# The first and third expert stage begin before the last six sequences are routed

## What is computed

```python
logits = x @ router_w
top_vals, top_idx = jax.lax.top_k(logits, K)          # K = 2 of 8 experts
importance = jax.nn.softmax(top_vals, axis=-1)
gate = jax.nn.silu(jnp.einsum('th,ehf->etf', x, w1))  # layer 1: F = 256
up = jnp.einsum('th,ehf->etf', x, w3)
expert_out = jnp.einsum('etf,efh->eth', gate * up, w2)
...
h = jax.nn.gelu(x @ W1[e] + b1[e])                    # layer 2: F = 512
y = h @ W2[e] + b2[e]
...
x = x + 0.5 * ffn0(layernorm(x));  x = x + attention0(layernorm(x));  x = x + 0.5 * ffn0(layernorm(x))
x = x + 0.5 * ffn1(x);             x = x + attention1(x);             x = x + 0.5 * ffn1(x)
```

## Time and profile before

| What | us |
|---|---|
| median of 3 runs (3025.21 to 3033.71) | 3025.9 |
| span of the profiled execution | 3022.4 |

### The profile page before, as it was taken

The page is one execution under the profiler, slowest core; times in us unless marked ns, Lnnn a source line. Parts: engine busy times, 40 slices in busy tenths (PEclk is TensorE's granted clock), DMA queues, the critical chain, the costliest instruction groups (busy, mean ns, idle before and its releaser), DMA issues.

```text
span 3022.4 us, 74232 instructions
## 1 busy us (share of the span) xinstructions
PE 2350.3 (78%) x24646; PEld 1530.8 (51%) x24646; DVE 2147.5 (71%) x6077; ACT 1635.4 (54%) x3371; POOL 1531.1 (51%) x1644
## 2 busy tenths in 40 slices
PE   2328958999999588532699489999999999958990
PEld 1217746777777477422588323333333333327880
DVE  3636657778776467686577488888888888846775
ACT  1116634555555366311577247777767667747770
POOL 4770034666653477577100555566565653145871
PEclk9999978999999799755799679999999999979995
DMA  8123323223322244332322111111111111012226
GB/s 171 43 64 104 104 68 88 81 79 80 84 79 59 57 116 119 98 96 71 90 87 84 60 47 40 39 49 52 40 47 47 47 37 44 19 33 77 86 85 177
DMA packets 250053, 222.84 MB, mean 74 GB/s; under 512 B 67078, under 2 KB 230668, under 8 KB 249164
## 3 DMA queue, kind: packets, MB, share of 16 engines
q1 hardware_dynamic: 216028, 148.82, 17.9%
q0 software_dynamic: 33664, 69.27, 7.6%
HBM read 114.00 MB, written 107.53 MB: 73 GB/s over the span
## 4 chain that ended last, share of the span: by engine, by line
PE 53%; POOL 14%; DVE 8%; issue 8%; ACT 4%; DMA 4%; SPq 1%; POOLq 0%; DVEq 0%; ACTq 0%
PE PS L525 10%; POOL choice_outputs L1116 8%; PE PS L705 8%; PE PS L529 6%; PE PS L674 6%; PE PS L653 6%; PE PS L616 5%; POOL slot_inputs L1107 4%; DVE xr L1268 3%; PE PS L723 2%; ACT arena L854 2%; PE PS L657 2%; PE PS L661 2%; DVE mxs L1494 2%; PE PS L682 1%
## 5 line engine op out<-in xcount | busy, mean ns | idle before, releaser
L964 ACT ACTIVATE arena<-PS 128x512 f32<-128x512 f32 (+1 forms) x1344 | 699.1, 586 | 284.7 <-PE PS L674 163.2
L1494 DVE TENSOR_REDUCE mxs<-PS 128x1 f16<-128x512 f32 x1024 | 650.6, 685 | 113.3 <-PE PS L653 103.4
L1107 POOL DMA_INDIRECT slot_inputs<-xs,slots x512 | 510.4, 997 | 414.1 <-PE PS L674 211.2
L1173 POOL DMA_INDIRECT G<-block_outputs,places x256 | 253.8, 991 | 654.7 <-DMA block_outputs<-arena 424.2
L653 PE MATMUL PS<-w,q 96*128 96x512 f16 x1024 | 398.8, 391 | 31.7 <-DVE mxs L1494 30.1
L674 PE MATMUL PS<-q,w 100*128 100x512 f16 x1024 | 390.6, 384 | 18.4 <-ACT arena L964 18.3
L1116 POOL DMA_INDIRECT choice_outputs<-arena x284 | 325.8, 1147 | 131.3 <-issue 83.0
L854 ACT ACTIVATE arena<-PS 128x256 f16<-128x256 f32 (+2 forms) x586 | 257.6, 440 | 225.4 <-PE PS L529 165.3
L529 PE MATMUL PS<-ident,arena 128*128 128x128 f32 x1084 | 204.1, 290 | 157.3 <-DMA arena<-slot_inputs 107.9
L1498 DVE TENSOR_REDUCE mxs<-PS 128x2 f16<-128x320 f32 x512 | 243.0, 492 | 117.3 <-PE PS L661 112.4
L1432 DVE TENSOR_TENSOR arena<-PS,arena 128x256 f16<-128x256 f32 x284 | 120.4, 424 | 238.0 <-ACT arena L854 238.0
(11 more groups left out here) (192 smaller groups left out, 4277.5 us busy)
## 6 DMA issues: line engine op xcount, KB each, us to landing
arena<-slot_inputs SPq DMA_DIRECT2D x284, 129.0 KB
block_outputs<-arena SPq DMA_DIRECT2D x142, 128.0 KB, 1.7
qk_parts<-qk SPq DMA_DIRECT2D x64, 256.0 KB, 2.4
G<-choice_outputs SPq DMA_DIRECT2D x64, 256.0 KB
q<-qk_parts SPq DMA_DIRECT2D x128, 96.0 KB
slot_inputs<-xs,slots POOLq DMA_INDIRECT x512, 2.4
qk_parts<-qk SPq DMA_DIRECT2D x64, 128.0 KB, 2.5
W<-qk_parts SPq DMA_DIRECT2D x128, 48.0 KB
```

The source lines that it names most:

```text
L964: activate(pT[:, u % PTR, 0:n], PS[:, SC0 + u % NSC[a], 0:n], ACT.Exp, scale=SCALE).then_inc(s_pe, 1)
L1107: g.indirect_dma_start(Xs, bass.IndirectOffsetOnAxis(ap=slots[:, s, c, k:k + 1], axis=0), xs[:, n % XSR, c if f % 2 else 0, k], None).then ...
L1173: g.indirect_dma_start(G[:, s % 2, k, c], None, Ys, bass.IndirectOffsetOnAxis(ap=places[:, s, c, k:k + 1], axis=0))\
L1494: vec.tensor_reduce(mxs[:, m % 2, p % NT, QROWS + col:QROWS + col + 1], PS[:, MX0 + u % NMX], AX, ALU.max)\
```

## The change

`routers(0)` and `routers(2)` now take only sequences 0 to 9 (`JOIN` = 10). When the slots of sequences 0 to 8 (`EARLY` = 9) are known, a first table (`full_blocks`) lists 29 blocks (`FULL` = 9 * 512 * 2 / 256 - 7) that these rows fill for certain. The expert stage begins with them as soon as the scatters of sequence 8 have landed. Sequences 10 to 15 are routed beside the blocks: sequence s starts in step 1 + 3(s - 10), and its parts k = 0 to 6 follow in one step each, so that every third step has k = 0 of one sequence with k = 3 and 6 of the two before, the next k = 1 and 4, the next k = 2 and 5 (k = 1 is empty). After the last part DVE lists the other 42 blocks (`other_blocks`, in step 22). SP pads, waits for that table and for all scatters before it loads block 29.

```diff
+            def beside(f, b):
+                if f % 2:
+                    return []
+                return [(s, b - 1 - APART * (s - JOIN)) for s in range(JOIN, SEQS) if 0 <= b - 1 - APART * (s - JOIN) <= 6]
...
 SP
             def ffn(f):
+                if f % 2 == 0:
+                    sp.wait_ge(*listed(f))
+                    rows_scattered(f, EARLY - 1)
+                else:
+                    rest_listed(f)
                 for b in range(NBLK + STLAG):
+                    if f == 2 and b < NBLK:
+                        for s in range(JOIN + 2, SEQS):
+                            if b == APART * (s - 2 - JOIN) + XRING + 3:
+                                fetch(1, s)
+                    if f % 2 == 0 and b == FULL:
+                        rest_listed(f)
...
 PE, after down(b - LAG)
+                def beside_block(b):
+                    for s, k in beside(f, b):
+                        if k == 2:
+                            if s > JOIN:
+                                pe.wait_ge(s_rpr, nth(f, s - 1))
+                            router_in(f, s, RB)
+                        if k == 3:
+                            router_logits(f, s, RB)
+                        if k == 4:
+                            pe.wait_ge(s_rlr, nth(f, s))
+                            router_positions(f, s, RB)
...
 ACT, after turned(b + 1)
+                def beside_block(b):
+                    for s, k in beside(f, b):
+                        if k == 3:
+                            router_inT(f, s, RB)
+                        if k == 5:
+                            router_exp(f, s)
...
 POOL, after routers(f)
+            def beside_ffn(f):
+                router_rstd(f, JOIN)
+                for s in range(JOIN, SEQS):
+                    scatter(f, s, 0, range(NT))
+                    if valid(s + 1):
+                        router_rstd(f, s + 1)
+                    scatter(f, s, 1, range(NT))
...
 DVE, after turned(b + 1)
+                def beside_block(b):
+                    for s, k in beside(f, b):
+                        if k == 0:
+                            if f:
+                                combine(f - 1, s)
+                                v.wait_ge(s_cmb, nth(f - 1, s))
+                            elif s % (SEQS // 4) == 0 or s == JOIN:
+                                v.wait_ge(s_xin[s // (SEQS // 4)], 16 * SEQS // 4)
+                            router_stats(f, s)
+                        if k == 2:
+                            router_norm(f, s)
+                        if k == 4:
+                            router_top(f, s, RB)
+                            router_places(f, s)
+                            router_diff(f, s)
+                        if k == 5:
+                            router_slots(f, s, RB)
+                        if k == 6:
+                            router_weights(f, s)
+                            if s == LASTS:
+                                other_blocks(f)
...
+                    if f % 2 == 0 and b > FULL and (b - FULL) % 8 == 0 and (b - FULL) // 8 <= SEQS // 4:
+                        rows_in_blocks(f, (b - FULL) // 8 - 1)
```

More of the change, by code:

```diff
@@ L46 @@
 STLAG = 12
+EARLY = 9
+APART = 3
 HALF = NG // 2
@@ L395, in _, with first_slot, rows_scattered, rest_listed @@
             sp.dma_start(brow[1:2], blo[:]).then_inc(s_br, 16)
-            def ffn(f):
-                sp.wait_ge(s_tab, 2 * f + 1)
+            def first_slot(f, b):
+                return sp.value_load(tabi[0:1, 0, b:b + 1], min_val=0, max_val=ROWS - BS)
+            def rows_scattered(f, s):
+                for c in range(2):
+                    for k in range(XSR):
+                        sp.wait_ge(s_scat[c][k], scattered(f * SEQS + s, k))
+            def rest_listed(f):
+                sp.wait_ge(s_cnt, f + 1)
                 for e in range(E):
@@ L497, in between @@
             def between(f):
-                for s in range(SEQS):
+                for s in range(JOIN + 2):
                     fetch(f, s)
@@ L564, in routers @@
             def routers(f):
-                for i in range(SEQS + 1):
+                for i in range(JOIN + 1):
                     if valid(i - 1):
@@ L1123, in routers @@
             def routers(f):
-                for i in range(-1, SEQS + 2):
-                    if valid(i + 1):
+                for i in range(-1, JOIN + 1):
+                    if i + 1 < JOIN:
                         router_rstd(f, i + 1)
@@ new lines, in other_blocks, with rows_in_blocks @@
+                n = NBLK - first
+                blocks_of(n, E - 1)
+                if first:
+                    link(vec.tensor_scalar(tbase[:], tdone[0:1, 0:1], float(BS), None, ALU.mult))
+                    link(vec.tensor_scalar(toff[:, 0:n], toff[:, 0:n], tbase[:], None, ALU.add))
+                list_blocks(f, first, n)
+                v.sem_inc(s_rest, 1)
+            def rows_in_blocks(f, i):
+                at = slots[:, 4 * i:4 * i + 4].rearrange("p s c k -> p (s c k)")
+                n = 8 * NT
+                link(vec.tensor_tensor(past, bcast(at, 2 * E), bcast(tfrom[:].rearrange("p e i -> p (e i)"), n, 1), ALU.is_ge))
+                link(vec.tensor_tensor(past, past, bcast(tjump[:], n, 1), ALU.mult))
@@ L1414, in routers @@
                         router_weights(f, i - 1)
+                    if i == EARLY:
+                        full_blocks(f)
                     if f == 0 and 3 <= i < 3 + len(big):
@@ L1462, in stored @@
                        .then_inc(s_yev, 1)
+                def beside_block(b):
[19 more added lines that the diff above has]
+                                other_blocks(f)
+                if f % 2:
+                    other_blocks(f)
                 turned(0)
-                if f % 2 == 0:
-                    rows_in_blocks()
                 for b in range(NBLK + LAG + 1):
```

190 lines of the change are left out of this document (123 added, 67 removed).

## The result

| | median, us | ratio to the kernel before, 95% interval |
|---|---|---|
| before | 3029.0 (5 runs) | |
| changed | 3046.5 (5 runs) | 1.0054 [1.0038, 1.0069] |

What follows compares the result with a forecast made beforehand. POOL's scatters bound the routings, PE the plain expert steps, DVE stage 3's routed steps. Terms -155.4 - 2.3 + 64.9 + 79.8 + 1 + 15 + 6 = +9.0 us gave 3035, range 2995 to 3065.

Steps and rivals of the forecast that it cites:

- The start: Blocks of stages 1 and 3 start after sequence 8's scatters, not sequence 15's: 77.4 and 78.0 us earlier.
- The wait: DVE idles before `router_norm` while POOL makes four scatters and `rrs`: 6.3 us, ten times, 63 us, covered by nothing.
- A: Stage 1 routed steps k = 0, 3, 6: PE's own 2.43 us plus logits of 1.84, together 4.3.
- B: Stage 1 routed steps with k = 4: DVE's 1.81 us plus the choice of experts, 1.75; with hops 3.7.
- C: Stage 1 routed steps k = 2, 5, with slots, POOL wait, norm and `router_in`: 10.8 us, or 3.7 without a wait.
- The steps of stage 3: DVE sets the steps beside stage 3's blocks: +79.8 us, three steps taking 23 us where they took 9.3.
- The clock: PE's matmuls run slow for a step after each idle wait in stages 1 and 3: +15 us (0 to +40).
- Rival 1: PE's clock stays at 1.2 GHz from step 4 to 23: 9 us more in stage 1, 16 in stage 3; 3060, chance 0.18.
- `other_blocks` and block 29: Listing the other blocks costs DVE 6.5 us a stage; block 29's loads arrive some 3.5 us early, costing 0.
- Rivals 3 and 4: 3: POOL has `rrs` before DVE asks, -63, 2972, chance 0.05. 4: block 29 late, some +10, 3045, chance 0.07.
- weights 1.7: DVE's router weights, nine small operations, 1.7 us of the 9.2 us a sequence adds in stage 3.
- Rival 2: Router work fills DVE's waits (-17), the clock recovers at once (-15), no gaps (-6): 2997 us, chance 0.20.

Runs made afterwards that it cites:

- e2_rrs_first: The changed kernel with POOL's `rrs` of the next sequence ahead of the scatters, not between their halves; 2967.6 us, ratio 0.9823 to the kernel before.
- e3_rrs_last: The changed kernel with POOL's `rrs` of the next sequence behind all eight scatters, not behind four; 3091.9 us, ratio 1.0244 to the kernel before.
- e8_fill: e1_exp4 with 22 unused matmuls ahead of `router_in` in each of the ten steps where PE waits for the norm; 3015.4 us, ratio 0.9973.
- e1_exp4: The changed kernel with attention 2's routing taking Exp as before, without the three added small DVE operations; 3022.3 us, ratio 1.0001 to the kernel before.
- e4_both: The changed kernel with `rrs` ahead of the scatters and attention 2's exponential without the three DVE operations; 2954.0 us, ratio 0.9771.

## Why the prediction was right, and where it wasn't

The range held the time and the direction was the likelier one, with 3035 forecast and 3046.5 measured. That is partly luck: a missing term of 18 was offset in part by terms that were too large. Point by point, for the two profiled executions:

- **The start.** Forecast -77.4 and -78.0, measured -74.6 and -77.7. In stage 1 the routing ran some 1.4 us later (the last scatter of sequence 8 ends at 148.7, not 147.35), and 5.8 us, not 4.4, lie between it and the first transposes. In the other kernels with an early first stage the transposes began at 149.7 to 152.5, so most of the 2.8 us is scatter between executions.
- **The wait.** Forecast 6.3 us, five times in each of the two stages, for four scatters and `rrs`; measured 6.30, 6.20, 6.22 in stage 1 and 6.32 in stage 3. No step of this chain failed, and e2_rrs_first and e3_rrs_last show that it is paid nearly in full. My choice of 0.96 us for a scatter also held: beside layer 2's blocks (1360 to 1490 us) they took 965 ns on average in the changed kernel. In e2_rrs_first, in which DVE doesn't rest, the average is 1140:

```profile
L1174 POOL DMA_INDIRECT slot_inputs<-xs,slots x48 | 54.7, 1140 | 37.0 <-DVE slots L1412 14.1 <-issue 12.8 <-DVE xs L1367 10.2
```

  The Trainium skill (GPSIMD Engine Reference, Key points) has GpSimd and VectorE share their SBUF interfaces; the pair 965 and 1140 agrees with it. But the median of these 48 is 960 ns: most scatters were as fast beside a busy DVE, and a few longer ones, up to 2012 ns, make the average.
- **The steps of stage 1.** Forecast for A, B, C: 4.3 (6.2 with the clock), 3.7, 10.8. Measured 5.25, 4.15, 10.35. A was too large because the logits were priced at 1.84 us, and they take 1.01 at 2.4 GHz. In e8_fill A takes some 3.1 us. The row came from routing 1, where the clock is low too, although the profile's table says 1.00: its transposes took 1.09 us, as after a wait. So I charged the low clock twice. The length of stage 1 was forecast as 186.9 + 64.9 - 1.3 + 11 + 3 + 0.5 = 265.0; measured 256.4. Six logits at 0.83 us too much are 5 of these 8.6 us.
- **The steps of stage 3.** DVE's sum held: 23 us for three steps forecast, 22.65 measured, and 227.2 + 79.8 - 1.0 + 4 + 3 + 0.5 = 313.5 us for the stage, 314.2 measured.
- **The clock.** +15 forecast, 11 in stage 1 and 4 in stage 3. The filled kernel gives 8.5 us by the ratios and 12.3 by the traces, 8.5 of them in the routed steps of stage 1, where its clock still fell after the last two waits. So the term was right in kind and near in size for stage 1. In the routed steps of stage 3 it shows 1 us. Rival 1, a low clock through all routed blocks, is refuted: B and C run at 1.47 us for the twelve `up`. Its counter-argument, that routing 1 shows 1.00 with as thin a load, was a misreading, and the sentence that the rows of routing 1 don't agree falls with it: by the durations routing 1 ran at the low clock.
- **`other_blocks` and block 29.** 6.5 us of DVE forecast, 6.9 measured (277.43 to 284.2). PE didn't wait for block 29 in either stage. Rivals 3 and 4 did not occur, and one bank in place of two cost nothing that a row shows.
- **The step that failed** is one that isn't in the sum: "weights 1.7" was counted in stage 3 only. The same function serves attention 2, where DVE is busy for 830.8 us of 1037 and PE for 917.1 and both wait for each other in turn, so that 0.85 us on the one comes out in the other. By itself it is 1.0066 and more than the whole measured difference. With it the same sum would have given 3035 + 12 to 18, 3047 to 3053. Without it, as e1_exp4 shows, the early start of the blocks comes out at no difference (1.0001), 9 us under my sum for it, a good half of which is the twice charged clock of stage 1.
- **Rival 2**, the faster case, was wrong in its reasons as they stood (A and B were not free), but the whole without the missing term lay between it and the forecast.

## What to carry to other kernels

When work is put beside a stage that runs in fixed order, the price is in the waits between its parts: here one small operation of POOL stood behind four slow ones that it didn't need, and its place in the list was worth 70 us of 3046. An edit to a helper has to be priced at every stretch that calls it, first of all at the one where the engine has least slack. And a duration taken from a stretch with a slow clock is not the price of the same work beside a busy PE.

## What the runs showed of the hardware

- Matmuls whose results nobody reads, put into ten waits of 6 to 7 us, made the kernel faster by 8.5 us. PE's granted clock rose from 0.82 to 0.96 over the routed part of stage 1, where PE sets the steps, and from 0.78 to 0.87 in stage 3, where DVE does and little was gained.
- The granted clock of a stretch at the start of the profile can read 1.00 where the durations say 1.2 GHz: the twelve `up` at 156.77 of the changed kernel took 2.76 us, in a stretch that reads 1.00, and the next twelve 1.47.

```profile
156.77 2.76 PE L567 MATMUL PS<-arena,w 128*128 128x256 f16 x12
159.63 1.47 PE L567 MATMUL PS<-arena,w 128*128 128x256 f16 x12
```
- 0.85 us more on DVE once a sequence cost 18 to 20 us over 16 sequences: 12 directly, and the rest in sequences in which a short rest of PE (1.62 us in the rows above) was followed by a stretch at half clock. The same work had such stretches three times in one execution and seven times in another (e1_exp4 and e4_both), 5.1 us apart.
